# Window attention, banded attention and a mixture of experts: expert outputs scattered back to token rows, tiles in two 256-row halves, nine groups of images in place of six

## The reference

```
x = x + shifted_window_attention(group_norm(x))       # 8x8 windows, shift 4, 8 heads, cosine scores, bias table, mask
t = tokens(x)                                         # 32 x 1024 rows of 128
t = t + banded_attention(layer_norm(t))               # windows of 128 tokens, 4 heads, band of 32 back
t = t + experts(layer_norm(t))
# experts: probs = softmax(x @ gate_w + gate_b); the two best of 8 experts e, each weighted by its probability:
#          y_e = gelu(x @ W1[e] + b1[e]) @ W2[e] + b2[e]        (128 -> 256 -> 128)
```

## Time and profile before

| | |
|---|---|
| median of three runs | 3094.0 us (3090.27 to 3098.82) |
| profiled execution, its span | 3088.7 us |
| TensorE busy | 2544.2 us (82%) |
| VectorE busy | 1965.5 us (64%) |
| GpSimd busy | 1914.2 us (62%) |
| ScalarE busy | 1865.7 us (60%) |
| DMA | 421.99 MB, 137 GB/s |

### The profile page before, as it was taken

One profiled execution on the slowest core, in us unless ns is written; L12 is line 12 of the kernel. 1 busy time (PEld: TensorE's weight loads), 2 busy tenths in 40 slices (PEclk: granted clock), 3 DMA queues, 4 the chain that ended last, 5 costly groups with the idle time before them and its releaser, 6 DMA issues.

```text
span 3088.7 us, 77036 instructions
## 1 busy us (share of the span) xinstructions
PE 2544.2 (82%) x27338; PEld 1794.8 (58%) x27338; DVE 1965.5 (64%) x5091; ACT 1865.7 (60%) x3409; POOL 1914.2 (62%) x2270
## 2 busy tenths in 40 slices
PE   6898889989888899889988988899888887676830
PEld 3565655556666666666666666666665665554520
DVE  4577777777666666777676676767776765522222
ACT  3666656666767677677776677767777654432310
POOL 1335555555444444576666576666667878779986
PEclk9998888888999999899999999999999988788965
DMA  5223333334445454144333343434343434456743
GB/s 208 104 110 117 117 132 150 147 127 138 147 173 182 161 183 161 60 148 123 100 122 117 107 144 122 126 96 127 119 149 111 131 109 135 123 171 203 244 127 91
DMA packets 262427, 421.99 MB, mean 137 GB/s; under 512 B 41740, under 2 KB 141080, under 8 KB 261280
## 3 DMA queue, kind: packets, MB, share of 16 engines
q1 hardware_dynamic: 219232, 327.69, 31.2%
q0 software_dynamic: 32768, 67.17, 7.7%
q10 hardware_dynamic: 10048, 22.19, 2.2%
HBM read 198.26 MB, written 231.22 MB: 139 GB/s over the span
## 4 chain that ended last, share of the span: by engine, by line
PE 48%; POOL 17%; ACT 15%; issue 10%; DVE 7%; DMA 2%; ACTq 1%; SPq 1%; POOLq 0%; DVEq 0%
PE bank_m L834 7%; POOL yg L1233 7%; PE bank_m L827 4%; PE bank_to L761 4%; POOL x_sorted L1223 4%; PE bank_s L801 4%; PE bank_s L807 3%; PE bank_s L716 3%; ACT pt_sb_a L1051 2%; POOL xin L1243 2%; PE bank_to L770 2%; PE bank_s L729 2%; ACT L1178 2%; ACT v_a L1036 2%; PE bank_s L739 2%
## 5 line engine op out<-in xcount | busy, mean ns | idle before, releaser
L1223 POOL DMA_INDIRECT x_sorted<-xn_c,place_i x512 | 534.3, 1044 | 282.1 <-PE bank_s L700 109.2
L1233 POOL DMA_INDIRECT yg<-y_sorted,place_i x512 | 521.4, 1018 | 241.1 <-PE bank_to L783 107.5
L1216 POOL TENSOR_TENSOR s_sb_a<-s_sb_a,mx_a 128x512 f32<-128x512 f32 x256 | 267.8, 1046 | 587.7 <-DVE mx_a L1607 586.9
L1599 DVE TENSOR_TENSOR s_sb_a<-bank_s,bias_a 128x512 f32<-128x512 f32 x256 | 176.6, 690 | 355.3 <-PE bank_s L700 257.7
L827 PE MATMUL bank_m<-xe,wk_e 128*128 128x512 f32 x552 | 280.5, 634 | 37.7 <-ACT hid L1084 27.7
L834 PE MATMUL bank_m<-wk_e,hid 128*128 128x128 f32 x2208 | 283.3, 291 | 0.9 <-ACT hid L1084 0.9
L834 PEld LDWEIGHTS bank_m<-wk_e,hid 128*128 128x128 f32 x2208 | 277.7, 208 | 2.2 <-issue 1.9
L1216 POOL TENSOR_TENSOR s_sb_b<-s_sb_b,mx_b 128x512 f32<-128x512 f32 x256 | 269.7, 1054 | 11.5 <-DVE mx_b L1607 11.5
L761 PE MATMUL bank_to<-k_consts,p_sb_b 128*128 128x128 f32 x1024 | 179.0, 300 | 92.2 <-ACT pt_sb_a L1051 56.1
L1051 ACT ACTIVATE pt_sb_b<-bank_to 128x512 f32<-128x512 f32 x256 | 152.5, 596 | 146.4 <-PE bank_to L761 145.7
L1207 POOL TENSOR_TENSOR km_a<-qk_a,k_consts 128x128 f32<-128x128 f32 x512 | 215.7, 445 | 40.0 <-DVE qk_a L1451 35.4
(11 more groups left out here) (221 smaller groups left out, 6266.7 us busy)
## 6 DMA issues: line engine op xcount, KB each, us to landing
y_sorted<-t_back SPq DMA_DIRECT2D x192, 512.0 KB, 5.5
y_sorted<-yo SPq DMA_DIRECT2D x170, 256.0 KB
wk_e<-in_w_experts_dram SPq DMA_DIRECT2D x134, 321.0 KB
xs<-x_sorted SPq DMA_DIRECT2D x134, 256.0 KB
t_kept<-t SPq DMA_DIRECT2D x64, 256.0 KB
t_back<-t_kept SPq DMA_DIRECT2D x32, 512.0 KB
xin<-in_x_dram SPq DMA_DIRECT2D x128, 112.0 KB
x_res<-in_x_dram SPq DMA_DIRECT2D x256, 56.0 KB
```

Source lines behind the costliest of these rows:

```text
L1216: pool.tensor_tensor(s[:, :, :], s[:, :, :], m[:, :, None].to_broadcast(shape), ALU.subtract).then_inc(s_sub[w], 1)
L1223: pool.indirect_dma_start(out=x_sorted[group_of[d] % XSIDES].ap(), out_offset=bass.IndirectOffsetOnAxis(ap=place_i[:, d, n:n + 1], axis=0) ...
L1233: pool.indirect_dma_start(out=yg[:, c % 2, n, :], out_offset=None, in_=y_sorted[side].ap(), in_offset=bass.IndirectOffsetOnAxis(ap=place_i ...
L1599: tt(s_sb[0][:, :, :].rearrange("p (r h) n -> p r (h n)", h=2), scores, bias_a[:, kind, :, :].rearrange("p (r h) n -> p r (h n)", h=2), AL ...
```

## The change

The sorted input row gets two columns more (130 in place of 128): HOME, the row number of its token in a new DRAM array y_tokens, and FIRST, its first-choice expert. `gate_choices` writes them with three VectorE operations more. After `slots_back` each tile's rows have a row number in back_to: HOME, plus one if the tile's own expert is not the token's first (`stt` with not_equal). GpSimd scatters the rows of yo, 128 at a time, straight to y_tokens (`scatter_back`), in which the two rows of a token lie side by side. So the gathers, `store_pair`, the fills and the memsets after indirect DMAs go; `bring_back` loads one image of y_tokens with one plain DMA of 1 MB. yo gets three buffers, and in the tail four buffers take turns for images.

A tile still has 512 rows, but consists of two halves of SLOTS = 256 that can belong to different experts: eight halves more than the rows need are planned for a group. Each half has its own rows, weights and DMAs. The padding rows come from a constant array, since they need a row number too. Two images may be summed in a pass from pass 16 on. Nine groups take the place of six. To make room, several buffers share memory, and some constants are loaded separately.

```diff
-GROUPS = (7, 7, 6, 5, 4, 3)
-SLOTS = 512
+GROUPS = (3, 4, 4, 4, 4, 4, 4, 3, 2)
+SLOTS = 256
+PART = 2
+YO, MOVES = 3, PART * SUB
+BACK_AT = (((4, 1), (4, 1), (4, 2), (4, 3), (4, 3), (5, 0), (5, 1), (5, 2)),
+           ((6, 1), (6, 2), (6, 3), (7, 1), (7, 2), (7, 3), (8, 0), (8, 1)),
+           ((9, 1), (9, 2), (9, 3), (10, 1), (10, 2), (11, 0), (11, 1), (11, 2)))
+OUT_AT = ((5, 0), (5, 2), (5, 3), (6, 0), (6, 1), (6, 2), (6, 3), (7, 0), (7, 1), (7, 2), (7, 3),
+          (8, 0), (8, 1), (8, 2), (8, 2), (8, 3))
-TWO_SUMS_FROM = 29
+TWO_SUMS_FROM = 16
...
-        tiles = list(range(TOP * size * TOKENS // SLOTS + E - 1))
+        tiles = list(range(0, TOP * size * TOKENS // SLOTS + SURPLUS, PART))
...
-                row = eng.value_load(tiles[0:1, kth:kth + 1], min_val=0, max_val=BUFFER - SLOTS)
...
-                eng.dma_start(wk_b[b], weights).then_inc(tile_in[b], 16)
+                for h in range(PART):
+                    at = kth + h
+                    row = eng.value_load(tiles[0:1, at:at + 1], min_val=0, max_val=BUFFER - SLOTS)
+                    expert = eng.value_load(tiles[0:1, MAX_TILES + at:MAX_TILES + at + 1], min_val=0, max_val=E - 1)
+                    rows = x_sorted[side].ap()[bass.ds(row, SLOTS), :].rearrange("(p j) d -> p (j d)", p=P)
+                    eng.dma_start(xs_b[b][:, h, :, :].rearrange("p j w -> p (j w)"), rows).then_inc(tile_in[b], 16)
+                    weights = w_experts[bass.ds(expert, 1), :, :].rearrange("e p n -> (e p) n")
+                    eng.dma_start(wk_b[b][:, h, :], weights).then_inc(tile_in[b], 16)
...
             def bring_back(c):
...
+                tiles_landed(sp, last_tile[group_of[c]])
...
+                sp.dma_start(y_home[home].rearrange("p t n d -> p (t n d)"),
+                             rows.rearrange("(p r) d -> p (r d)", p=P)).then_inc(y_in[home], 16)
...
-                    mm(banks[:, ch, :], w[:, P * ch:P * ch + P], xe[:, m, :], start=True, stop=True).then_inc(z_ready, 1)
+                    for h in range(PART):
+                        own = slice(SLOTS * h, SLOTS * h + SLOTS)
+                        last = mm(banks[:, ch, own], w[:, h, P * ch:P * ch + P], xe[:, m, own], start=True, stop=True)
+                    last.then_inc(z_ready, 1)
...
-                    func(hid[:, CH * m + ch, :], banks[:, ch, :], ACT.Gelu,
-                         bias=w[:, B1_AT + ch:B1_AT + ch + 1]).then_inc(gelu_ready, 1)
+                    for h in range(PART):
+                        own = slice(SLOTS * h, SLOTS * h + SLOTS)
+                        last = func(hid[:, CH * m + ch, own], banks[:, ch, own], ACT.Gelu,
+                                    bias=w[:, h, B1_AT + ch:B1_AT + ch + 1])
+                    last.then_inc(gelu_ready, 1)
...
+            def scatter_back(u, k):
+
+                _, q, _ = pairs[u].members[k // MOVES]
+                if k % MOVES == 0:
+                    pool.wait_ge(yo_ready, q + 1)
+                j = k % MOVES
+                pool.indirect_dma_start(out=y_tokens[pairs[u].group].ap(),
+                                        out_offset=bass.IndirectOffsetOnAxis(ap=back_to[:, q % YO, j:j + 1], axis=0),
+                                        in_=yo[:, q % YO, j, :], in_offset=None).then_inc(y_out[q % YO], 16)
...
                 def moves(k):
 
+                    for j in (i - 1, i):
+                        at = (t + TILES * (i - j), k)
+                        for slot in range(SLOTS_PER_PASS):
+                            u = slots[j][slot] if 0 <= j < PASSES else None
+                            if u is not None:
+                                for m, when in enumerate(BACK_AT[slot][0:MOVES * len(pairs[u].members)]):
+                                    if when == at:
+                                        scatter_back(u, m)
+                        if on(j - 3):
+                            for row, when in enumerate(OUT_AT):
+                                if when == at:
+                                    scatter(j - 3, row)
...
-                after(dve, y_out[q % 2], 16 * (q // 2))
-                tt(yo[:, q % 2, :, :], banks[:, m, :].rearrange("p (j d) -> p j d", j=SUB),
-                   w[:, None, B2_AT:B2_AT + D].to_broadcast([P, SUB, D]), ALU.add).then_inc(yo_ready, 1)
+                after(dve, y_out[q % YO], 16 * MOVES * (q // YO))
+                for h in range(PART):
+                    stt(back_to[:, q % YO, SUB * h:SUB * h + SUB], rows[:, h, :, FIRST], w[:, h, OWN_AT:OWN_AT + 1],
+                        rows[:, h, :, HOME], ALU.not_equal, ALU.add)
+                tt(yo[:, q % YO, :, :].rearrange("p (n j) d -> p n j d", n=PART),
+                   banks[:, m, :].rearrange("p (n j d) -> p n j d", n=PART, j=SUB),
+                   w[:, :, None, B2_AT:B2_AT + D].to_broadcast([P, PART, SUB, D]), ALU.add).then_inc(yo_ready, 1)
...
-            for c in range(first_tail_sum, IMAGES):
-                for k in range(TOP * TILES):
-                    gather(c, k)
-                    if c < IMAGES - UNPAUSED:
-                        apart()
+            for u in tail:
+                for k in range(MOVES * len(pairs[u].members)):
+                    scatter_back(u, k)
```

More of the change, by code:

```diff
@@ L119, in shape_constants @@
     put("base", rows(REGION * e))
+    put("experts", rows(e))
+    put("home", TOP * (SPARE + TILES * ch[:, None] + np.arange(TILES)[None]))
     img = np.zeros((SIDE, SIDE), np.int32)
@@ L499, in load_residual @@
                                      x_rolled[a, r, c0:c1, tiles, :]).then_inc(xr_in[h], 16)
-            def store_pair(u):
-                pair = pairs[u]
-                side, tiles = pair.group % YSIDES, table[pair.group % TABLES]
-                if pair.group >= YSIDES:
-                    sp.wait_ge(summed, SUM_STEPS * (last_image[pair.group - YSIDES] + 1))
-                else:
-                    sp.wait_ge(filled[side], 16 * FILLS)
-                for m, q, kth in pair.members:
-                    sp.wait_ge(yo_ready, q + 1)
-                    row = sp.value_load(tiles[0:1, kth:kth + 1], min_val=0, max_val=BUFFER - SLOTS)
-                    rows = y_sorted[side].ap()[bass.ds(row, SLOTS), :].rearrange("(p j) d -> p (j d)", p=P)
-                    sp.dma_start(rows, yo[:, q % 2, :, :].rearrange("p j d -> p (j d)")).then_inc(y_out[q % 2], 16)
             def spill(c, h):
@@ L1300, in _ @@
                     step(i, t)
-            for k in range(12, TOP * TILES):
-                scatter(IMAGES - 1, k)
-                apart()
-            for c in sums[PASSES - 1][1:]:
-                for k in range(12, TOP * TILES):
-                    gather(c, k)
-                    apart()
-            for c in range(first_tail_sum, IMAGES):
-                for k in range(TOP * TILES):
-                    gather(c, k)
-                    if c < IMAGES - UNPAUSED:
-                        apart()
+            for row, (t, _) in enumerate(OUT_AT):
+                if t >= TILES:
+                    scatter(IMAGES - 1, row)
+            for u in tail:
+                for k in range(MOVES * len(pairs[u].members)):
+                    scatter_back(u, k)
         @block.vector
@@ L1592, in biased @@
+                    tt(rows[:, :, 0, :], rows[:, :, 0, :], t2_home[kept], ALU.add).then_inc(summed, 1)
             def biased(w, n):
```

328 lines of the change are left out of this document (153 added, 175 removed).

## The result

The changed kernel takes 3204.9 us (median of four runs, 3194.4 to 3210.7), the kernel before 3092.1 in the same session: a ratio of 1.037, with a 95% interval of 1.0325 to 1.0415. The forecast was 3058, with a range that ended at 3140.

A forecast was written before the change was run, and what follows sets the result against it. No one engine bounds the run: TensorE paces steady passes, GpSimd late passes, its 192 gathers the tail. Passes +121, late -27, tail -130 sum to -36: 3053, plus 5.3 for the median, 3058 us; range 2960 to 3140.

The forecast's parts named there:

- The step that failed: GpSimd inside passes: 5.5 us late after the seventh and eighth steps, taken as 2.5 in each of 24 passes, +60.
- Theory 1: Follow-up explanation: seven and eight moves between two subtractions make GpSimd the pace there (bunching).
- 91 as a sign of being wrong: Passes with three pairs: starts some 88 us apart would show the forecast right, 85 or 91 wrong.
- GpSimd only 55 of 84: Steady passes with three pairs: TensorE busy 75 to 79 us, GpSimd only 55, so TensorE sets the pace.
- The light steps: Steps after the seventh and eighth, with 3, 3 and 2 moves: a reason to price less than 5.5 us a pass.
- The price of seven moves: Seventh step: seven moves need 11.4 us, where the step lasted 9.4; eight need 12.7 in the next.
- GpSimd paces all passes with pairs: Slower rival: the whole 5.5 us is paid in 24 passes, 3151 us; decides from 4.0 a pass; chance 0.26.
- Halves: Expert pairs up to pass 30: two 256-column gelus for one of 512, 0.23 us of ScalarE a pair, +14.
- The start of a group: First tile loads of seven groups, passes 6 to 30: some 7 us each with TensorE stopped, +49, bounds 0 and 70.
- Pairs and two-sum passes: Up to pass 30: 60 pairs in place of 59, +5; two summed images stop costing 48 moves, about -7.
- Late passes: From 2441.7 to 2737.2 us: GpSimd's list has 40 moves a pass and no pauses, -27, bounds 0 and -60.
- Tail: Last expert work to the end: thirteen pairs, 14.5 us from copy to copy, 221.5 for 351.5 us, -130.

The follow-up runs named there:

- bunched kernel: Kernel before the change, with only an image's 16 scatters placed 1, 7 and 8 in three steps instead of four in each of four: 3240.7 us, ratio 1.0507.
- Spreading the moves: Changed kernel with the same 40 moves a pass put at other steps: 6, 6, 6, 5, 5, 4, 4, 4 between subtractions; 3089.9 us, ratio 1.0027.
- fitted kernel: Changed kernel with its 40 moves a pass placed to suit the steps' lengths, 6, 5, 4, 4, 5, 6, 6, 4: 3044.9 us, ratio 0.9872.
- fitted six groups: The fitted kernel with six groups of 7, 7, 6, 5, 4, 3 images in place of nine groups: 3017.4 us, ratio 0.9777.
- whole tiles: Fitted kernel with six groups, its tiles made 512 rows for one expert instead of two halves of 256: 3004.9 us, ratio 0.9756.
- whole-tile kernel with tail loads on SP: Fitted six-group kernel with 512-row tiles for one expert and the tail's loads issued on SP's queue instead of ScalarE's: 3018.9 us, ratio 0.979.
- one expert in the first layer: Fitted kernel with both halves of a tile using the first half's first-layer weights and bias, 512-column matmuls and gelu: 3021.4 us, ratio 0.9795.

## Why the prediction was wrong

**The step that failed** is "I take 2.5 us in each of the 24 passes to pass 30 that have pairs: +60, bounds 0 and 132". Theory 1 stands: two kernels show it from opposite sides, the bunched kernel before (+149 us) and the changed kernel with its moves fitted (-160). To the cast of pass 30 the placing of the moves cost 2694.3 - 2530.9 = 163 us, 6.8 a pass, beyond even the upper bound. In the table of steps the seventh and eighth alone grew by 4.0 and 3.2. The passes with three pairs last 92 to 99 us (before pass 30), where the prediction named 91 as a sign of being wrong. Four things were wrong in it:

- *Busy time was read as slack.* "GpSimd only 55 of 84" leaves out the 0.30 us ahead of each move and the order of its list. The earlier trace rows had the true slack: 1.0 to 1.2 us at the end of a step with four moves, not quite room for one more. In steps of 9 us a move beyond that lengthens the step.
- *The light steps gave nothing back.* Where the step after has no move, it does (bunched kernel: 9.6 to 6.6 in the table). In the changed kernel the step after has five moves and gives back 0.5, and the fifth step, with seven moves that the sum did not price, grew by 1.3. The second and fourth grew by 1.7 and 1.6 though light, and there GpSimd is not the pace: it waits for VectorE's maximum, in pass 23 8.53 us ahead of the fifth step's subtraction (the line below). TensorE is, busy 12.0 of 12.6 us and 11.6 of 12.7 (means over passes 7 to 29; 10.4 and 10.5 before), while in the first step it is busy only 5.9 in place of 8.3. That this is work put off from the first step fits, but is not shown. Spreading the moves took some 0.8 of each away.

```profile
2039.77 1.03 POOL L1244 TENSOR_TENSOR s_sb_a<-s_sb_a,mx_a 128x512 f32<-128x512 f32 x1 [8.53 <-DVE mx_a L1617]
```

- *The price of seven moves was a floor.* Eight took 12.8 on average, as the 12.7 forecast; seven took 13.0 and not 11.4. Passes 7 to 29 show two lengths of this step: 12.2 us in the eleven in which VectorE sums no image during it, 14.0 in the eleven in which it does (pass 9 has no pairs and 10.2). The masks take 1.3 and 2.3 us in them and the seven moves 7.0 and 7.8, as in the timeline above: masks 2.26 in place of 0.76, and one scatter 1.81.
- *Only waiting was priced.* The changed and the fitted kernel run the same 27786 matmuls, yet TensorE is busy 86 us longer in the changed one, half of the 172 us between the two spans (one execution each). From the two pages, changed and fitted:

```profile
PE 2611.7 (81%) x27786; PEld 1998.1 (62%) x27786; DVE 2128.5 (66%) x5551; ACT 1907.0 (59%) x3721; POOL 1950.9 (61%) x2197
```
```profile
PE 2525.8 (83%) x27786; PEld 1929.8 (64%) x27786; DVE 2078.6 (68%) x5551; ACT 1901.7 (63%) x3721; POOL 1949.4 (64%) x2197
```

From 500 to 2440 us TensorE's mean granted clock is 0.89 in the changed kernel, 0.93 in the fitted and 0.94 before, so more of the stretch ran at the lower of its two levels, 1.2 in place of 2.4 GHz, while TensorE stood still more often. This goes with the placing in every execution: over the whole run the mean is 0.881 to 0.889 in the changed kernel and 0.886 to 0.889 in the bunched one, 0.905 to 0.910 in the fitted one and 0.907 to 0.916 before (in the session of the bunched and the fitted). The sum has no term for it. That the clock is the whole of the 86 us is not shown.

The rival "GpSimd paces all passes with pairs" had the right mechanism, and its point of decision, 4.0 us a pass, was passed; its size, 5.5 a pass, was still too small.

**The other terms.** The +252.6 us up to the cast of pass 30 come apart by four kernels, each difference from one profiled execution:

| part | from | us |
|---|---|---|
| placing of the moves | changed 2694.3 - fitted 2530.9 | 163.4 |
| nine groups for six | fitted - fitted six groups 2492.4 | 38.5 |
| halves for whole tiles | six groups - whole tiles 2452.6 | 39.8 |
| scattering back, moves fitted | whole tiles - before 2441.7 | 10.9 |

The two lower rows are good to some 20 us: the whole-tile kernel with tail loads on SP runs the same passes, and its cast of pass 30 is at 2470.6, 18 us later, which would make them 21.8 and 28.9. And the rows depend on the order: with the moves left bunched, six groups in place of nine move the cast by 79.4, and with six groups the placing costs 122.6 (2614.9 - 2492.4). Nine groups have pairs in 24 passes to pass 30, six in 20.

*Halves* (+14, bounds 0 and 104): one expert in the first layer moves this cast by 19 us on the fitted kernel (2530.9 to 2511.9), so the term was near, partly by luck: over the whole run the gelus of the fitted kernel are busy 264.6 us and those with one expert 219.2, some 0.55 us for each of the 82 pairs and not 0.23, and of these 45 us 23 came off the time. The whole price of halves is more. The row of 39.8 (21.8 by the other profile) has five pairs fewer on its left side; at the prediction's 4.7 us a pair that makes it some 63 (45) for 54 pairs. What makes up the rest (twice the loads, their issue, waits for weights) stays open.

*The start of a group* (+49): in the stretch shown TensorE waited 18.6 us for weights, at most 4.8 at once, and not 7 at each start. What nine groups cost besides (six further pairs, pairs in four more passes) is not separated.

*Pairs and two-sum passes* (+5, -7) were not measured by themselves.

*Late passes* (-27): -19.

*Tail* (-130): -113. The copies into xe start at 2972.57, 2981.19 and so on to 3163.81. Leaving out the one across the last group's start (26.4 us), the ten from the second on are 15.6 us apart, for 14.5 forecast; that start cost 10.9 for 14; and 45.0 us follow the last copy, for 37.9. The mechanism, ScalarE's gelus queued behind its load issues, is what the trace shows; but it does not bind alone: with the loads on SP the fitted six-group kernel's tail shrinks by 9 us, and TensorE waits for weights instead. The Trainium skill's rule that the prediction weighed (DMA: Bandwidth & Descriptors, Anatomy of one DMA — SWDGE (gpsimd) path) gives the time of one DMA, a fixed 2.0 us and its bytes at 436 GB/s. Read as the pace of a queue it would have put the tail at an estimated 290. As a pace the trace disagrees with it: scatters in the tail start 1.26 us apart (3171 to 3187 us).

## What to carry to other kernels

When moves on a queue are rearranged, count them between two points at which another engine waits for that queue, and compare with the wait that the timeline shows at such a point; neither the sum over a pass nor the busy share tells what one more costs. A step's slack is the bracket in front of the waiting instruction, and every move beyond it costs its whole issue distance unless the very next step is left nearly empty. Waits are not the whole price either: here about half of it showed as the same matmuls taking longer. When a change brings several edits, the placing of the same work is worth trying alone: here it decided between 3.7% slower and 1.3% faster.

## What was not expected of the hardware

VectorE's row number operation of 128x2 took 0.22 us in the tail and up to 2.78 in the passes. The timelines of VectorE and GpSimd after the change, at one such place (the first line is two of these operations, of 2.56 and 0.21 us):

```profile
514.75 2.69 DVE L1580 SCALAR_TENSOR_TENSOR back_to<-xs,wk_e 128x2 uint32<-128x2 f32 x2 [0.82 <-PE bank_m L860]
517.37 0.68 DVE L1582 TENSOR_TENSOR yo<-bank_m,wk_e 128x512 f32<-128x512 f32 x1
```
```profile
515.24 1.06 POOL L1244 TENSOR_TENSOR s_sb_a<-s_sb_a,mx_a 128x512 f32<-128x512 f32 x1
516.24 1.05 POOL L1244 TENSOR_TENSOR s_sb_b<-s_sb_b,mx_b 128x512 f32<-128x512 f32 x1
```

The two end 0.15 us after GpSimd's second subtraction, at 517.44 and 517.29. It goes the other way too: while GpSimd's masks of pass 23 took 2.26 us (2068.40 to 2070.66), VectorE added two 1024-column operands of an image's sum from 2068.99 to 2070.41. The Trainium skill (SBUF — State Buffer, SBUF: two separate sides) says that a VectorE operation with two SBUF inputs and a GpSimd operation that reads SBUF exclude each other for the whole instruction, and the trace agrees with it at these two places. So moving GpSimd's work to other steps also changes what it collides with: the seventh step's 12.2 us without an image's sum and 14.0 with one put what goes with the sums at 1.8 us in about half of the passes, some 0.9 of the 4.0 us by which the step grew.
